# Cross attention: two of four tiles' exponentials transposed by DMA

## What is computed

```python
x = x + attn(layernorm(x))           # self attention over the 4 rows (T = 4, 16 heads of 32), causal
x = x + xattn(layernorm(x), ctx)     # cross attention, 16 heads of 32, over 128 context tokens
x = x + ffn(layernorm(x))            # 512 -> 64, a sum of 16 hinges per feature, 64 -> 512
# in xattn:
scores = einsum('bnlh,bnph->bnlp', qm, km) / sqrt(32)
out = einsum('bnlp,bnph->bnlh', softmax(scores), vm) @ Wo.T + bo
```

## Time and profile before

| | |
|---|---|
| median of three runs | 1782.7 us |
| profiled execution, its time | 1784.44 us |
| profiled execution, its span | 1782.6 us |
| PE busy | 1685.4 us (95%) |
| DVE busy | 1514.8 us (85%) |
| ACT busy | 1069.8 us (60%) |
| POOL busy | 1017.6 us (57%) |
| DMA, queue 1 | 17.0% of 16 engines' span |
| mean granted clock of PE | 0.983 |

### The profile page before, as it was taken

How to read it: one execution, slowest core, us unless ns; L and a number is a source line. 1 busy time by engine, 2 the same in 40 slices (tenths; PEclk the granted TensorE clock), 3 DMA queues, 4 the chain that set the end, 5 groups by cost and what they waited for, 6 DMA issues and landing times.

```text
span 1782.6 us, 37666 instructions
## 1 busy us (share of the span) xinstructions
PE 1685.4 (95%) x13824; PEld 1392.6 (78%) x13824; DVE 1514.8 (85%) x2089; ACT 1069.8 (60%) x3420; POOL 1017.6 (57%) x721
## 2 busy tenths in 40 slices
PE   6899999999999999997799999999999999999996
PEld 5678888888888888885677787778777787777874
DVE  6788888888888888787678898888988899888886
ACT  4434444444443334442767788777877788777884
POOL 3267766666666666695554464545654465544521
PEclk9999999999999999998799999999999999999998
DMA  5410111111111111044201112011111112011101
GB/s 210 128 42 25 47 48 48 47 47 47 47 47 47 47 47 47 2 107 79 68 8 51 62 62 63 25 62 62 63 38 43 62 62 69 19 62 62 39 20 54
DMA packets 72793, 98.75 MB, mean 55 GB/s; under 512 B 22208, under 2 KB 30528, under 8 KB 72640
## 3 DMA queue, kind: packets, MB, share of 16 engines
q1 hardware_dynamic: 72064, 96.63, 17.0%
q10 hardware_dynamic: 576, 0.07, 0.0%
HBM read 59.66 MB, written 37.03 MB: 54 GB/s over the span
## 4 chain that ended last, share of the span: by engine, by line
PE 28%; ACT 12%; DVE 8%; issue 4%; DVEq 0%; POOL 0%; ACTq 0%; POOLq 0%
PE ring L1464 11%; ACT prob_c L1679 10%; DVE g_sb L1794 5%; PE sc L1492 5%; PE ring L1504 3%; PE ring L1469 3%; PE ring L1549 3%; PE sc L1484 2%; PE sc L1464 1%; DVE q_first L1975 1%; ACT relu L1660 1%; DVE g_sb L1791 1%; DVE gT L1803 1%; ACT gT L1669 1%; ACT pT L1648 0%
## 5 line engine op out<-in xcount | busy, mean ns | idle before, releaser
L447 PE MATMUL qb<-wqkv,xT 128*128 128x512 f32 x2304 | 551.9, 393 | 6.1 <-DVE wqkv L1016 6.1
L447 PEld LDWEIGHTS qb<-wqkv,xT 128*128 128x128 f32 x2304 | 429.7, 189 | 93.7 <-DVE wqkv L1016 6.3
L1679 ACT ACTIVATE prob_c<-sc,ntop 128x128 f32<-128x128 f32 x1024 | 362.6, 390 | 22.1 <-DVE ntop L1821 18.7
L1410 POOL TENSOR_TENSOR rstd<-vare,half_c 128x1 f32<-128x1 f32 x64 | 35.1, 549 | 433.6 <-DVE vare L1875 433.6
L1679 ACT ACTIVATION_READ_ACCUMULATOR prob_c<-sc,ntop 128x1 f32 x1024 | 236.1, 231 | 0.0
L352 POOL TENSOR_TENSOR prod_pool<-v,prob 128x1024 f32<-128x1024 f32 x64 | 179.9, 2810 | 67.8 <-DVE prob L911 62.6
L1464 PE MATMUL ring<-wqkv,aT_c 128*128 128x512 f32 x768 | 194.5, 402 | 8.0 <-DVE aT_c L1778 7.1
L663 ACT ACTIVATE v<-qb 128x512 f32<-128x512 f32 x64 | 38.3, 598 | 259.9 <-PE qb L447 249.6
L583 PE MATMUL ob<-wout,aT 128*128 128x512 f32 x768 | 191.4, 398 | 0.8 <-DVE aT L941 0.8
L1821 DVE TENSOR_REDUCE ntop<-sc 128x4 f32<-128x512 f32 x256 | 173.3, 683 | 12.3 <-PE sc L1492 9.5
L663 ACT ACTIVATE qk<-qb 128x512 f32<-128x512 f32 x128 | 76.1, 595 | 175.8 <-PE qb L447 175.8
(11 more groups left out here) (152 smaller groups left out, 3358.5 us busy)
## 6 DMA issues: line engine op xcount, KB each, us to landing
x_tile<-in_x SPq DMA_DIRECT2D x16, 1024.0 KB, 5.2
x_scratch<-xres SPq DMA_DIRECT2D x16, 1024.0 KB, 4.6
x_tile<-x_scratch SPq DMA_DIRECT2D x16, 1024.0 KB, 5.3
out<-x SPq DMA_DIRECT2D x64, 256.0 KB, 2.0
kt<-k_scratch SPq DMA_DIRECT2D x16, 512.0 KB, 3.2
v_c<-v_scratch SPq DMA_DIRECT2D x16, 256.0 KB, 3.6
raw<-in_wqkv SPq DMA_DIRECT2D x3, 1024.0 KB, 8.9
ctx<-in_ctx SPq DMA_DIRECT2D x1, 1024.0 KB, 8.3
```

The source lines that it names most:

```text
L447: last = nc.tensor.matmul(qb[g % 4][:, :], xT[p][a][:, k, t * P:(t + 1) * P], wqkv[b][:, k, c * D:(c + 1) * D], start=(n == 0), stop=(n == ...
L1679: last = nc.scalar.activation(prob[:, h, :], sc[g][:, (h % 4) * C:(h % 4 + 1) * C], ACT.Exp, bias=ntop[:, h:h + 1], accum_out=total[:, t % ...
```

## The change

Tiles 2 and 3 of each step are no longer transposed by PE. ACT copies eight heads of their exponentials at a time to fp16 (`part_hi`, into p16_0), the low part goes to p16_1 (`part_lo`), and SP issues a DMA transpose of each of the four pieces (part 0 and 1, high and low) into pT (`turn`, 256 KB each). The low parts of tile 2 are made by POOL, after residual(1), those of tile 3 by DVE: part 0 behind norm_lo(1), part 1 behind the last query's low part, at the end of the step. pT is now a pair of buffers. p16 is written again only when the transposes that read it have landed (`turned`). exps(3, g) and the next exps(0, g) wait for the low parts instead of for transposes.

The exponentials no longer accumulate. The values get a column of ones per head (33 columns per product), so the sums come out of the value product; normalise takes their reciprocal from PSUM, after values. That result takes two adjacent ring banks (`value_sums`, `ring_places`).

In PE's list, out_proj(3) moves behind norm_T(0), ffn_out(3) and norm_T(1), and values(3) behind norm_T(3). On SP, the four transposes of tile 2 stand ahead of load_ctx, the fourth store moves into its own step behind load_ctx, and the four transposes of tile 3 come last. aT and gT move into free columns of the weight tile. Two semaphores are merged into others.

```diff
+VW = DH + 2
-            vparts = sb0("vparts", [P, R, 2, D], F16)
+            vparts = sb0("vparts", [P, R, 2, H, VW], F16)
...
+            nc.vector.memset(vparts[:, :, :, :, DH:VW].rearrange("p r a h e -> p (r a h) e"), 0.0).then_inc(v_ones, 1)
+            dve.wait_ge(v_ones, 1)
+            nc.vector.memset(vparts[:, :, 0, :, DH:DH + 1], 1.0).then_inc(v_ones, 1)
...
     late = [("pT", 4 * t - 2), ("pT", 4 * t - 1)]
     if t < 3:
-        return [("aT", t)] + late + [("out", t), ("wo", t), ("pv", t), ("x2T", t), ("pT", 4 * t), ("pT", 4 * t + 1)]
-    return ([("aT", 3), ("xT", 0)] + late + [("wo", 3), ("xT", 1), ("out", 3), ("pv", 3), ("xT", 2), ("xT", 3),
-            ("pT", 12), ("pT", 13), ("x2T", 3)] + [("q", m) for m in range(DK)] + [("pT", 14), ("pT", 15)])
+        return ([("aT", t)] + late + [("out", t), ("wo", t), ("pv", t), ("x2T", t)]
+                + ([("pT", 4), ("pT", 5)] if t == 1 else []))
+    return ([("aT", 3), ("xT", 0), ("out", 3), ("xT", 1), ("wo", 3), ("xT", 2), ("xT", 3), ("pv", 3), ("x2T", 3)]
+            + [("q", m) for m in range(DK)])
...
+def ring_places():
+
+    place, user, n = {}, {}, 0
+    for turn in RING:
+        width = 2 if turn[1] == "pv" else 1
+        if n % 4 + width > 4:
+            n += 1
+        place[turn] = n
+        for at in range(n, n + width):
+            user[at] = turn
+        n += width
+    return place, user
...
+            def turn(j, t, part):
+
+                m = 2 * j + t - 2
+                heads = slice(8 * part, 8 * part + 8)
+                for h in range(2):
+                    if h == 0:
+                        wait(sp, p_hi, 2 * m + part + 1)
+                    else:
+                        wait(sp, p_lo[t - 2], 2 * j + part + 1)
+                    wait(sp, psum["pv"], 4 * j + t - 1)
+                    sp.dma_start_transpose(pT[t % 2][h][:, heads, :],
+                                           p16[h][:, heads, :].rearrange("p h c -> p (h c)")).then_inc(turned[part], 16)
...
-                if active(j - 1, "out", 3):
-                    store(j - 1, 1 - p, 3)
                 for t in range(R - 1):
                     if active(j, "out", t):
                         store(j, p, t)
+                if has(j):
+                    turn(j, 2, 0)
+                    turn(j, 2, 1)
                 if has(j, 1):
                     load_ctx(j + 1, 1 - p)
+                if active(j, "out", 3):
+                    store(j, p, 3)
+                if has(j):
+                    turn(j, 3, 0)
+                    turn(j, 3, 1)
...
+                part_lo(2, 0)
+                part_lo(2, 1)
                 norm2(j, 3)
...
                 def values(t, j=j):
-                    wait(pe, taken["pT"], 4 * over)
+                    n = over - 1
+                    if n % 4 < 2:
+                        wait(pe, taken["pT"], TURNS_OVER["pT"](n // 4, 4 * (n % 4) + 3))
+                    n_dma = 2 * (n // 4) + n % 4 - 2 if n % 4 >= 2 else None
...
                     for h in range(H):
+                        head = head_of(h)
+                        if n_dma is not None and h % 8 == 0:
+                            wait(pe, turned[h // 8], 32 * (n_dma + 1))
...
+                            last = nc.tensor.matmul(dst[:, head // 8, head % 8, :], pT[n % 2][a][:, h, :],
+                                                    v[:, pp, b, head, 0:DH + 1],
+                                                    start=(i == 0), stop=(i == 2))
...
                 scores(3)
                 attn_T(3)
                 norm_T(0)
-                prob_T(10)
-                prob_T(11)
+                ffn_out(3)
+                norm_T(1)
                 out_proj(3)
-                norm_T(1)
-                ffn_out(3)
-                values(3)
                 norm_T(2)
                 norm_T(3)
-                prob_T(12)
-                prob_T(13)
+                values(3)
...
+                def part_hi(t, part):
+
+                    m = 2 * j + t - 2
+                    heads = slice(8 * part, 8 * part + 8)
+                    wait(act, exped, 16 * j + 4 * t + 2 * part + 2)
+                    wait(act, turned[part], 32 * m)
+                    nc.scalar.activation(p16[0][:, heads, :], prob[:, heads, :], ACT.Copy).then_inc(p_hi, 1)
...
+                part_hi(2, 1)
+                attn_hi(3)
+                norm2_hi(2)
+                exps(3, 0)
+                norm_hi(0)
+                exps(3, 1)
+                part_hi(3, 0)
+                norm_hi(1)
+                exps(3, 2)
+                exps(3, 3)
                 norm_hi(2)
                 norm_hi(3)
-                prob_hi(j, 12)
-                prob_hi(j, 13)
+                part_hi(3, 1)
...
+                tops(3, 0)
+                attn_lo(3)
+                tops(3, 1)
+                norm2_lo(2)
+                norm_lo(0)
+                tops(3, 2)
+                add_out(3)
+                tops(3, 3)
+                norm_lo(1)
+                part_lo(3, 0)
+                add_attn(3)
+                statistics(3)
                 norm_lo(2)
                 norm_lo(3)
-                prob_lo(j, 12)
-                prob_lo(j, 13)
+                normalise(3)
...
                 for m in range(DK):
                     hinges(*HINGE_RUNS[m])
...
+                part_lo(3, 1)
```

More of the change, by code:

```diff
@@ L1223 @@
 RING = [(j, kind, i) for j in range(TILES) for kind, i in TURNS
-        if active(j, kind, i) and (j, kind, i) not in ENDING] + ENDING
-PLACE = {turn: n for n, turn in enumerate(RING)}
+        if (j, kind, i) not in ENDING] + ENDING
+def ring_places():
[9 more added lines that the diff above has]
+    return place, user
+PLACE, USER = ring_places()
 def bank_of(j, turn):
@@ L1235, in head_of, with banks_before @@
     return 4 * (slot % 4) + slot // 4
-def bank_before(j, turn):
-    at = PLACE[(j, *turn)] - 4
-    if at < 0:
-        return None
-    step, kind, i = RING[at]
-    return kind, TURNS_OVER[kind](step, i)
-CROSS_SMALL = [("kt", [P, 2, DK, C], F32R), ("fillrows", [P, C], F32R), ("v_c", [C, 2, 2, D], F16),
+def banks_before(j, turn):
+    first = PLACE[(j, *turn)]
+    found = []
+    for at in range(first, first + (2 if turn[0] == "pv" else 1)):
+        at -= 4
+        while at >= 0 and (at not in USER or not active(*USER[at])):
+            at -= 4
+        if at >= 0 and USER[at] not in found:
+            found.append(USER[at])
+    return [(kind, TURNS_OVER[kind](step, i)) for step, kind, i in found]
+CROSS_SMALL = [("kt", [P, 2, DK, C], F32R), ("fillrows", [P, C], F32R), ("v_c", [C, 2, 2, H, VW], F16),
                ("bo", [P, D], F32), ("bf", [P, D], F32), ("hinge", [P, 3, PAIRS], F32), ("bin", [P, 1], F32),
@@ L1453, in bank @@
             def bank(j, turn):
-                before = bank_before(j, turn)
-                if before:
-                    wait(pe, taken[before[0]], before[1])
+                for kind, over in banks_before(j, turn):
+                    wait(pe, taken[kind], over)
                 return ring[bank_of(j, turn)]
```

167 lines of the change are left out of this document (88 added, 79 removed).

## The result

The changed kernel takes 1796.3 us (median of four runs, 1794.96 to 1800.57), against 1782.7 us before: a ratio of 1.0082, 95% interval 1.0064 to 1.0101. It is slower by 13.6 us; the forecast was 7 us faster. The profiled execution has a span of 1795.2 us (before: 1782.6).

What follows compares the result with a forecast made beforehand. TensorE, busy 95% of the span, was taken as the bound, with other engines close behind. Terms of -1.14 and +0.75 gave -0.39 per step, -5.9 over 15 steps, -7 with the last step: 1776 us, range 1752 to 1810.

Steps and rivals of the forecast that it cites:

- tile 0, without the transpose: First tile: without the accumulator read exponentials come every 0.25 us, so the 0.64 wait at scores(1) goes; -0.64 per step.
- tile 1: Second tile: keeps its transposes; prob_T(5) waits for normalise(1), so nearly all of the 0.24 wait stays; 0.
- tile 2: Third tile: its last transposes go, but scores(3) waits for exponentials behind add_attn(2) and the reductions; -0.55 per step.
- tile 3 to ffn_in: Fourth tile: the ring and part_lo(3,0), taken as 1.75 us, hold TensorE; ffn_in at 11.9 against 11.39, +0.5.
- ffn_in to scores(0): Step's end: GpSimd's norm(0) and norm(1) move off the hinges, so ffn_out(0) comes earlier; -0.55, between 0 and -0.95.
- value products: All tiles: 33 columns for 32 cost at most 0.04 us per tile; +0.1 per step.
- last transpose: Step's start: tile 3's last transpose lands late for values(0); +0.75 us per step.
- GpSimd: Two low parts of about 2.5 us each per step and later-loaded norms, covered by 1.1 us before norm2_T(1); no cost.
- X: Time from issue to landing of one 256 KB DMA transpose, taken as 2.8 us; forecast wrong if over 3.3.
- rival C: Effects cancel: X of 2.9 to 3.5, or exponentials' pitch stays near 0.34; about 1782 us, chance 0.15.
- each us counts: At values(0): landing time up to 2.05 us is free; beyond it each us counts, through values(0), normalise(0) and out_proj(0).
- Rival B: The last transpose becomes the wait at values(0), outweighing savings from X = 3.2; +1.5 per step, 1805 us, chance 0.3.

Runs made afterwards that it cites:

- e10: The changed kernel with only the last query's low part on VectorE moved between the first two pairs of hinges: 1771.1 us, ratio 0.9926.
- e8: The changed kernel with only x2T(2)'s high and low parts taken earlier, ahead of attn_hi(3) and tops(3,0): 1804.3 us, ratio 1.0132.
- e7: e1 with TensorE made to wait in the middle of values(0) for VectorE's tops(0,1): 1809.8 us, ratio 1.0159.
- e1: The changed kernel with the last query's low part made directly after normalise(3), ahead of the hinges: 1771.5 us, ratio 0.9930.
- e3: The changed kernel with x2T(2)'s parts taken earlier and add_attn(3) ahead of the low part of the fourth tile's first half: 1766.7 us, ratio 0.9901.
- e9: The changed kernel with e3's order and the last query's low part moved between the first two pairs of hinges: 1761.2 us, ratio 0.9859.
- e12: e10 with out_proj(3) back directly behind norm_T(0) and add_attn(3) directly behind tops(3,3): 1763.5 us, ratio 0.9898.
- e11: e9 with the last query's low part made by GpSimd at the end of its list, not by VectorE: 1806.4 us, ratio 1.0136.
- e4: The changed kernel with the exponentials accumulating their sums again, into a tile that nobody reads: 1860.7 us, ratio 1.0429.

## Why the prediction was wrong

The prices of the parts hold, within 0.2 us each but for the low part in the fourth tile; what was missing is a term. For a quiet step, against before:

| place | forecast | measured | from |
|---|---|---|---|
| tile 0, without the transpose | -0.64 | -0.72 | 8.14 in e10, 8.86 before |
| tile 1 | 0 | +0.18 | 10.09, 9.91 |
| tile 2 | -0.55 | -0.42 | 9.49, 9.91 |
| tile 3 to ffn_in | +0.5 | +0.07 | 11.46, 11.39 |
| ffn_in to scores(0) | -0.55 | -0.49 | 16.43, 16.92 |
| value products | +0.1 | 0 | 1.36 for 48, as the earlier trace rows |
| last transpose | +0.75 | +0.81 | 8.95 after, 8.14 in e10 |
| sum | -0.39 | -0.57 | 56.45 - 56.98 = -0.53 |

**Tile 0.** Right: the wait at scores(1) is gone, and the exponentials come at a pitch of 0.26 (0.25 taken).

**Tile 1.** prob_T(5) waits 0.32. The prediction had it wait for normalise(1); the trace names ScalarE's exponentials, which end at 1206.89, and normalise(1) ends at 1206.84, so either would hold it. The tile is 0.18 longer than before, where 0 was forecast.

**Tile 2.** scores(3) waits 0.74; 0.6 was forecast.

**Tile 3.** The wait at norm_T(1) is 1.62 (1.5 forecast) and values(3) waits for what stands behind part_lo(3,0); e8 shows that the second wait alone sets the time. The term that was mis-sized is that low part: 1.75 was taken between bounds of 1.15 and 2.49, and the trace has both ends and nothing between, 1.22 in ten of steps 2 to 14 and 2.35 in three, as GpSimd's addition comes after or before it. The fourth tile is 11.46 or 12.6, the forecast's own bounds being 11.3 and 12.65. Its mean is +0.34 against before, so +0.5 was not far off in the mean.

**The end.** Right in size and cause: norm(0) starts in the next step, the pair of hinges takes 1.6.

**GpSimd.** Its low parts take 2.14 each, not 2.5; norm(0) starts at t = 8.9 and norm2_T(1) does not wait.

**The last transpose.** The issue comes at t = 0.95 and the wait ends at 4.11, 3.2 us later; X was taken as 2.8. The queue of SyncE and the landings in one step:

```profile
L1408 SPq DMA_TRANSPOSE pT<-p x8: 1232/1270/2179, 1188.1 to 1228.8; - x8
...
DMA to landing us min/median/max: 3.1/3.2/4.6
```

An issue holds SyncE for 1.23 to 2.18 us where the earlier trace rows has 0.38 for a plain one; I had counted 0.38 for each of the eight. In four of 13 steps X is larger, and those landings add 0.24 us to the mean step. By that alone X comes to about 3.4 on the average, a little over the 3.3 beyond which the text called itself wrong. The sum would be -0.53 + 0.24 = -0.29 per step, and with the low part's mean (+0.27) -0.02: no gain and no loss, the time of rival C though not by its causes.

**The step that failed** is the sentence that beyond X = 2.05 "each us counts", as if a wait of TensorE cost its own length. It costs more. Behind a wait of 1.1 us and up in values(0) the granted clock fell to 0.50 in six of 13 steps, and the products behind it lost another 1.2 to 1.5 us, 2.5 once. With two falls behind values(3) that is 0.93 us in the mean step, a term that the sum had at nothing. -0.29 + 0.27 + 0.93 = +0.91 per step; measured is 57.88 - 56.95 = +0.93. Steps 2 to 14 so make 12.1 of the 12.6 us by which the span grew. Of the rest, the start and step 0 are 3.5 us shorter, step 1 is 2.8 longer, and the last step, of which the prediction took 1 us off, is 1.1 longer. Before the change no wait of TensorE in a step was over 0.64, and the clock stayed at 1.00 in all of them. Rival B named the right wait but gave it the wrong price: it wanted X = 4.2 or more for +1.5.

That the fall comes from the idle time and not from the DMA traffic is shown by e7 against e1 (one wait more, nine falls more) and by the two steps with equal traffic; that removing the wait gives back more than its length, by e1 and e10: their first tile is 1.76 us shorter in the mean, of which the transpose's own delay is 1.05. Not settled is why a wait of the same length is sometimes followed by a fall and sometimes not. 1.1 us in values(0) was in three of nine steps of the changed kernel and in none of nine in e3; 1.57 in values(0) in nine of 13 (e7), about as much ahead of ffn_out(0) in four of 14 (e9), 1.62 at norm_T(1) in none of 13, and 1.97 at values(3) in two of three. So the length alone doesn't decide it. Nor was e3's order tried on e12, or the load of the next rows held back in e11.

## What to carry to other kernels

A wait of the busiest engine can cost more than its length. Here every fall of the clock in the changed kernel's steps 2 to 14 stood behind a wait of TensorE of 1.1 us or more and cost about as much again; so price such waits above their length, and look in the timeline whether the same products take longer behind them. Where the operations of two engines slow each other and come due at nearly the same time, look at all the steps and not at one: the traced step showed the good order, and three of 13 had the other. Where a DMA takes over the work of an engine, put what feeds it (here one low part of 1.2 us) early enough that the landing is hidden with a margin; one line moved turned a loss of 0.8% into a gain of 0.7%. And of several waits in a row remove all or none: half of e3 took 0.1 us off the fourth tile and left one longer wait with the clock falling behind it, the whole took 1.6 off.

## What the runs showed that was not expected

The accumulator read of the exponentials costs 0.08 us a head, but 64 us over the kernel when TensorE waits for it (e4 against the changed kernel). A DMA transpose holds the issuing queue for 1.23 us or more and lands 256 KB in 3.0 to 5.9 us (median 3.6; a plain store of that size takes 2.1, and the load of v_c of 272 KB, which stands behind others, 4.3). The Trainium skill (Advanced Engine Details and Errata, X-Bar Transpose) has such transposes as fast as regular DMAs; against the store the trace does not agree. Work moved to an idle GpSimd took 2.6 us from VectorE to save it 1.2 (e11).
